# First batch of x in two halves, low weight parts of two more heads on VectorE, other banks for two chunks, later norms of x

## What is computed

```python
def ln(x): return (x - mean(x)) / sqrt(var(x) + 1e-5)          # over the 256 columns

n = ln(x)                                                       # x: (4, 256, 256)
q, k, v = (einsum('bim,mhd->bhid', n, w) for w in (wq, wk, wv)) # 16 heads of 128
q, k = rope(q), rope(k)
p = softmax(q @ k.T / 128 - 1e30 * (i < j))
x = x + ln(einsum('bhid,hdm->bim', p @ v, wo))
h = ln(x)                                                       # 1024 rows
r, chosen = top_k(h @ router.T + router_bias, 4); w = softmax(r)
gate, up = (h @ gate_up[e] + b)[0::2], [1::2]                   # for each chosen expert e
gate, up = min(gate, 7), clip(up, -7, 7)
y = sum over e of w[e] * ((up + 1) * gate * sigmoid(1.702 * gate) @ down[e] + down_bias[e])
x = x + ln(y)
```

## Time and profile before

| | us |
|---|---|
| median of 3 runs | 497.1 |
| lowest and highest | 496.76, 497.86 |
| the profiled execution | 498.67 |
| its span (first to last instruction) | 496.7 |
| PE busy in it | 470.8 |
| DVE, ACT, POOL busy | 359.4, 326.9, 240.9 |

### The profile page before, as it was taken

One profiled execution on the slowest core, in us unless ns is written; L12 is line 12 of the kernel. 1 busy time (PEld: TensorE's weight loads), 2 busy tenths in 40 slices (PEclk: granted clock), 3 DMA queues, 4 the chain that ended last, 5 costly groups with the idle time before them and its releaser, 6 DMA issues. The chain is left out here.

```text
span 496.7 us, 11704 instructions
## 1 busy us (share of the span) xinstructions
PE 470.8 (95%) x3482; PEld 439.7 (89%) x3482; DVE 359.4 (72%) x1263; ACT 326.9 (66%) x815; POOL 240.9 (49%) x228
## 2 busy tenths in 40 slices
PE   7799999999999999999999999998699999999993
PEld 4698899999999999999999998887589999999983
DVE  3798799687876677787678698577367778866735
ACT  4878986767676777667678566675256765665612
POOL 2888785435323256344453236115435565665612
PEclk9999999999999999999999999999799999999998
DMA  8367751999300000001365346631275665776462
GB/s 255 105 197 231 227 175 49 373 368 370 108 1 1 23 14 37 36 14 38 131 221 197 128 145 215 204 88 71 46 160 93 103 97 98 116 123 79 46 188 86
DMA packets 61661, 65.26 MB, mean 131 GB/s; under 512 B 4960, under 2 KB 56480, under 8 KB 61600
## 3 DMA queue, kind: packets, MB, share of 16 engines
q1 hardware_dynamic: 53008, 53.44, 33.6%
q0 software_dynamic: 7872, 10.49, 12.7%
q10 hardware_dynamic: 720, 0.59, 0.4%
HBM read 31.58 MB, written 32.92 MB: 130 GB/s over the span
## 5 line engine op out<-in xcount | busy, mean ns | idle before, releaser
L527 POOL TENSOR_TENSOR by_sin<-by_sin,rope_sin 128x512 f32<-128x512 f32 x64 | 82.8, 1294 | 139.9 <-ACT by_sin L649 139.9
L1343 PE MATMUL bank<-xT_parts,qk_h 128*128 128x256 f32 x512 | 99.6, 293 | 3.8 <-POOL qk_l L512 1.6
L1544 PE MATMUL bank<-xgT,gu_now 128*128 128x128 f32 x752 | 94.1, 279 | 7.2 <-DVE gu_now L1146 6.3
L1544 PEld LDWEIGHTS bank<-xgT,gu_now 128*128 128x128 f32 x752 | 89.4, 195 | 8.9 <-DVE gu_now L1146 7.0
L649 ACT ACTIVATE by_sin<-bank 64x512 f32<-64x512 f32 x128 | 75.9, 593 | 31.8 <-PE bank L1343 29.0
L625 POOL DMA_INDIRECT sum_d<-y,xg x44 | 69.9, 1589 | 55.0 <-ACT y L777 35.8
L1343 PEld LDWEIGHTS bank<-xT_parts,qk_h 128*128 128x128 f32 x512 | 79.1, 191 | 5.0 <-POOL qk_l L512 2.4
L671 ACT ACTIVATE prob<-score,row_bias 128x128 f32<-128x128 f32 (+1 forms) x128 | 57.0, 447 | 26.7 <-DVE row_bias L974 26.4
L1343 PE MATMUL bank<-xT_parts,qk_l 128*128 128x256 f32 x256 | 72.4, 283 | 0.0
L1343 PE MATMUL bank<-wv_h,xT_parts 128*128 128x256 f32 x256 | 66.6, 324 | 1.5 <-ACT V L649 1.4
L964 DVE TENSOR_TENSOR qkT<-bank,by_sin 128x512 f32<-128x512 f32 x64 | 44.3, 692 | 18.0 <-POOL by_sin L527 15.3
(11 more groups left out here) (183 smaller groups left out, 1061.2 us busy)
## 6 DMA issues: line engine op xcount, KB each, us to landing
rows_d<-blank SPq DMA_DIRECT2D x32, 576.0 KB, 7.2
gu_w<-_L_ffn_gate_up_proj_dram SPq DMA_DIRECT2D x16, 512.0 KB
xg<-rows_d SPq DMA_DIRECT2D x47, 144.0 KB, 2.5
dn_w<-in_L_ffn_down_proj_dram SPq DMA_DIRECT2D x16, 256.0 KB
raw_qk<-in_L_attn_wq_dram SPq DMA_DIRECT2D x16, 128.0 KB, 3.6
raw_qk<-in_L_attn_wk_dram SPq DMA_DIRECT2D x16, 128.0 KB, 3.7
raw_v<-in_L_attn_wv_dram SPq DMA_DIRECT2D x8, 256.0 KB, 2.9
raw_o<-in_L_attn_wo_dram SPq DMA_DIRECT2D x16, 128.0 KB, 2.7
```

The lines of the kernel that those rows point to most:

```text
L527: pool.tensor_tensor(v, v, rope_sin[:, :].unsqueeze(1).broadcast_to([P, 2, T]), ALU.mult).then_inc(pool_sin, 1)
L1343: m = pe.matmul(out, lhs, rhs, start=first and i == 0, stop=last and i == len(terms) - 1, skip_group_check=not (first and last))
L1544: m = pe.matmul(ps_gu[i][:, (2 * s + r) * P:(2 * s + r + 1) * P], gu_now[:, i % 2, k, s, r * P:(r + 1) * P], xgT[:, i % XT, k, :], start=( ...
```

## The change

1. Batch 0 of x is loaded by two DMAs, one for each tile. Statistics, power, norm, transpose, high part and low part are done for each tile by itself, with two banks (`ps_first`). On ACT, `high_qk(0)` stands between the two norms. PE's fillers at the start are two products of 512 columns and one of 256, and two and three products of 128 columns behind the transposes of the halves.
2. `DVE_HEADS` is 4: DVE makes the low parts of wq and wk for heads 2 and 3 too.
3. Chunks 2 and 3 go to banks 7 and 6, and chunks 4 and 5 wait for `rotate(0)` and `rotate(1)`, where chunks 2 to 5 waited for `rotate(0)` to `rotate(3)`.
4. ACT's, POOL's and DVE's orders in the start are other ones. In the slots, POOL does `low_v` ahead of `low_o`.
5. The statistics of batches 1 to 3 of x are taken in slots 5, 10 and 12 (`X_SLOTS`), and ACT normalises them in slots 6, 11 and 13.

```diff
-        ps_qk = bank[0:2]
+        ps_qk = [bank[0], bank[1], bank[7], bank[6]] + [bank[n % 2] for n in range(4, SLOTS)]
...
+        ps_first = [ps_s, ps_pT]
...
-        DVE_HEADS, DVE_PAIRS = 2, 1
+        DVE_HEADS, DVE_PAIRS = 4, 1
+
+        X_SLOTS = (5, 10, 12)
...
-            load_x(0)
+            for s in range(2):
+                sp.dma_start(x[:, s, :], x_rows[:, s, :]).then_inc(dma_first_x[s], 16)
...
             pool.wait_ge(dma_rope, 32)
             times_sine(0)
             times_sine(1)
-            low_qk(3)
+            low_qk(4)
+            times_sine(2)
             low_v(1)
-            times_sine(2)
-            low_qk(4)
+            times_sine(3)
             low_qk(5)
-            times_sine(3)
             low_o(0)
...
                 if b == 0:
+                    if h % 2 == 1 and h // 2 + 2 < H // 2:
+                        low_v(h // 2 + 2)
                     if h + 1 < H:
                         low_o(h + 1)
-                    if h % 2 == 1 and h // 2 + 2 < H // 2:
-                        low_v(h // 2 + 2)
-                    if h in (1, 2, 3):
-                        power("x", h)
+                    if h in X_SLOTS:
+                        power("x", X_SLOTS.index(h) + 1)
...
-            normalise("x", 0, xn, x)
+            first_norm(0)
             high_qk(0)
-            sc.wait_ge(pe_xT, 1)
-            copy(xT_h[:, 0, :, :], ps_s[:, :].rearrange("p (k t) -> p k t", k=KM)).then_inc(act_xT, 1)
+            first_norm(1)
+            first_xT_high(0)
+            first_xT_high(1)
             high_qk(1)
             high_v(0)
             high_qk(2)
             swap(0)
             high_qk(3)
             swap(1)
+            high_qk(4)
             values(0)
+            swap(2)
             high_v(1)
-            swap(2)
-            high_qk(4)
+            softmax_exp(0)
             swap(3)
+            softmax_exp(1)
             high_qk(5)
-            softmax_exp(0)
-            softmax_exp(1)
...
-                    if h in (4, 5, 6):
-                        normalise("x", h - 3, xn, x)
+                    if h - 1 in X_SLOTS:
+                        normalise("x", X_SLOTS.index(h - 1) + 1, xn, x)
...
-                if n >= 2:
-                    pe.wait_ge(dve_rope, n - 1)
+                if n >= 4:
+                    pe.wait_ge(dve_rope, n - 3 if n < 6 else n - 1)
...
-            keep_busy(qkT[:, 0, 0, 0:P], qkT[:, 0, :, :].rearrange("p w t -> p (w t)"), 4)
+            keep_busy(qkT[:, 0, 0, 0:P], qkT[:, 0, :, :].rearrange("p w t -> p (w t)"), 2)
+            keep_busy(qkT[:, 0, 0, 0:P], qkT[:, 0, 0, :], 1)
             pe.wait_ge(dma_ident, 16)
-            pe.wait_ge(act_norm, 1)
-            turn_rows(0, ps_s).then_inc(pe_xT, 1)
+            for s in range(2):
+                pe.wait_ge(act_first_norm[s], 1)
+                for k in range(KM):
+                    m = pe.transpose(ps_first[s][:, k * P:(k + 1) * P], xn[:, s, k * P:(k + 1) * P], ident[:, :])
+                m.then_inc(pe_first_xT[s], 1)
+                keep_busy(qkT[:, 0, 0, 0:P], qkT[:, 0, 0, 0:P], 2 + s)
```

More of the change, by code:

```diff
@@ L209, in block_kernel @@
         ps_sum = bank[6:8] + bank[0:2]
-        dma_x = [sem(f"dma_x{u}") for u in range(4)]
+        ps_first = [ps_s, ps_pT]
+        dma_x = [None] + [sem(f"dma_x{u}") for u in range(1, 4)]
+        dma_first_x = [sem(f"dma_first_x{s}") for s in range(2)]
         dma_ident = sem("dma_ident")
+        dve_first_var = [sem(f"dve_first_var{s}") for s in range(2)]
+        dve_first_mean = [sem(f"dve_first_mean{s}") for s in range(2)]
+        pool_first_rstd = [sem(f"pool_first_rstd{s}") for s in range(2)]
+        pool_first_shift = [sem(f"pool_first_shift{s}") for s in range(2)]
+        act_first_norm = [sem(f"act_first_norm{s}") for s in range(2)]
+        pe_first_xT = [sem(f"pe_first_xT{s}") for s in range(2)]
+        act_first_xT = [sem(f"act_first_xT{s}") for s in range(2)]
         dma_rope = sem("dma_rope")
@@ L268, in block_kernel @@
         dve_var = sem("dve_var")
+        dve_mean = sem("dve_mean")
         dve_xT = sem("dve_xT")
@@ L317, in block_kernel @@
         pe_y = sem("pe_y")
-        NORMS = ([("x", u) for u in range(B)] + [n for u in range(B) for n in (("a", u), ("b", u))]
+        NORMS = ([("x", u) for u in range(1, B)] + [n for u in range(B) for n in (("a", u), ("b", u))]
                  + [("moe", u) for u in range(B)])
@@ L561, in tables @@
                     pool.memset(tile_edge[:, 0:1], -1.0).then_inc(pool_table, 1)
-            power("x", 0)
-            low_qk(2)
+            for s in range(2):
+                pool.wait_ge(dve_first_var[s], 1)
+                pool.tensor_tensor(first_rstd[:, s:s + 1], first_eps[:, s:s + 1], minus_half[:, 0:1], ALU.pow).then_inc(pool_first_rstd[s], 1)
+                pool.wait_ge(pool_first_rstd[s], 1)
+                pool.wait_ge(dve_first_mean[s], 1)
+                pool.tensor_tensor(first_shift[:, s:s + 1], first_mean[:, s:s + 1], first_rstd[:, s:s + 1], ALU.mult).then_inc(pool_first_shift[s], 1)
             pool.wait_ge(dma_rope, 32)
@@ L1175, in _, with first_stats, first_xT_low @@
             dve.memset(qkT[:, 0, :, :], 0.0).then_inc(dve_idle, 1)
-            dve.wait_ge(dma_x[0], 16)
-            row_stats(x, "x", 0)
+            def first_stats(s):
+                dve.wait_ge(dma_first_x[s], 16)
+                chain(dve.bn_stats(stats[:, s, :], x[:, s, :]))
+                chain(dve.bn_aggr(mean_var[:, s, :], stats[:, s, :]))
+                dve.tensor_scalar(first_eps[:, s:s + 1], mean_var[:, s, 1:2], EPS, None, ALU.add).then_inc(dve_first_var[s], 1)
+                dve.tensor_scalar(first_mean[:, s:s + 1], mean_var[:, s, 0:1], -1.0, None, ALU.mult).then_inc(dve_first_mean[s], 1)
+            def first_xT_low(s):
+                dve.wait_ge(act_first_xT[s], 1)
+                cols = slice(s * P, (s + 1) * P)
+                m = dve.tensor_tensor(xT_l[:, 0, :, cols], ps_first[s][:, 0:KM * P].rearrange("p (k t) -> p k t", k=KM),
+                                      xT_h[:, 0, :, cols].bitcast(F32), ALU.subtract)
+                if s == 1:
+                    m.then_inc(dve_xT, 1)
+            first_stats(0)
+            first_stats(1)
             low_qk(0)
-            xT_low(0, ps_s)
+            first_xT_low(0)
+            first_xT_low(1)
             low_qk(1)
             low_v(0)
+            low_qk(2)
             dve.wait_ge(dma_rope, 32)
             cosine(0)
+            low_qk(3)
             rotate(0)
@@ L1190, in _ @@
             cosine(2)
+            row_max(1)
+            normalise_prob(0)
             rotate(2)
             cosine(3)
-            row_max(1)
-            normalise_prob(0)
             rotate(3)
```

39 lines of the change are left out of this document (27 added, 12 removed).

## The result

The changed kernel takes 495.42 us, median of 8 runs (494.51 to 496.18); the kernel before took 497.25 beside it, median of 8 (496.14 to 499.24). The ratio is 0.9959, with a 95% interval of 0.9945 to 0.9974: 1.3 to 2.7 us less. The forecast was 493.0, a gain of 4.1 us; the measured gain is 1.8. The sign was right, and 495.42 lies within the stated range, near its upper end. The profiled execution of the changed kernel took 495.41, with a span of 493.4.

The account below looks back on a forecast made before the run. TensorE was taken as the bound, busy 95% of the span, so only its waits could be won. 1.95 us from the start plus 2.1 from the ten slots gave 4.05 off the 497.1 median: 493.0 us, range 491.4 to 495.9.

Parts of the forecast that it names:

- What bounds the kernel: Whole kernel: TensorE is busy 95% of the span, so only time in which it waits can be won.
- First product, 0.15 earlier: Start of attention: PE's first product at 9.75 instead of 9.91 us, between 0.35 later and 0.9 earlier.
- weigh_values(0) at 23.7: End of the start: first weigh_values 2.15 us before 25.85, with ACT as bound; bounds 1.3 and 2.8.
- Slots 1 and 2, 1.95 left: Slots 1 and 2: weigh_values(2) ends at 34.3 instead of 36.2, keeping 1.95 of the start's 2.15 us.
- Order on POOL and later norms, 2.1 us: Ten slots from 38.00 to 87.01: low_v first and later norms win 2.1 of 3.1 us of waits; bounds 0 and 3.1.
- The ring: Two-slot wait cycle through single buffer raw_v over ACT and POOL: 10.2 us against PE's 9.0, falling to 8.5.
- The range: Whole kernel's time: 491.4 to 495.9 us.
- the start's lower bound: Least gain at the first weigh_values, 1.3 us, from more ACT waits for weights; total given as 495.9.
- Rival B, the clock: Start: thinner warm-up leaves PE at the lower clock, losing 1.25 to 2.1 us; 494.7 us, chance 0.20.
- Rival C: Slots: waits for raw_v stay, as ACT or its load is late; only 1.95 us won, 495.1, chance 0.13.
- Rival D: Expert stage: one more PE hold of 4.3 us with its cold stretch; slower, 500.4 us, chance 0.08.
- Rival E: No change: worst cold start (2.1) together with raw_v waits that stay; 0.15 earlier, 497.0 us, chance 0.09.

Follow-up runs that it names:

- halves_alone: Kernel before with only the first batch of x normalised and turned as two halves, and the shorter fillers; ratio 1.0009 to the kernel before.
- start_alone: Kernel before with four heads on DVE, chunks 2 and 3 in banks 7 and 6, and the new orders ahead of the slots; ratio 1.0053.
- ring_undone: Changed kernel with POOL's low_o put back ahead of low_v in the slots; ratio 0.9960 to the kernel before.
- norms_early: Changed kernel with the norms of x back at statistics in slots 1, 2, 3 and ACT's part in 4, 5, 6; ratio 0.9966 to before.
- start_and_ring: Kernel before with four heads on DVE, banks 7 and 6, the new start orders, and low_v ahead of low_o in POOL's slots; ratio 0.9959.
- norms_in_batch_1: Changed kernel with the second and third norms of x later: statistics in slots 14 and 20, ACT's part in 15 and 24; ratio 0.9918 to before.
- change_again: The changed kernel run once more, with no edit; ratio 0.9965 to the kernel before.
- later_and_no_double: Changed kernel with second and third norms at slots 14/15 and 20/24, and slot 10's qk_l of head 15 behind the sine product; ratio 0.9933.

## Why the prediction was right or wrong

**What bounds the kernel: right.** What the edits moved, they moved before 90 us, and the distance from slot 13 to the last scores was the same in each of fourteen traces: a lead at slot 13 was kept whole.

**First product, 0.15 earlier: mis-sized, without effect.** It came 1.00 us earlier (9.71 to 8.88 in the traces of the change's start at the full clock with halves, against 9.91). The forecast took wk's landing at its slowest, 5.4 us after an issue at 1.75, thus 7.15. Behind the additional load of x it was issued at 2.17, and high_qk(0) could start at 6.27; in the second trace it waited until 7.07. The first norm was forecast at 5.45, from an arrival at 3.5 that mixes a time with durations counted from the issue at 0.73; the half was there by 3.32 and the norm started at 5.17. The bound of 0.9 was given. But the term was not in the sum, as ACT was the bound, and halves_alone confirms that.

**weigh_values(0) at 23.7: right.** 23.67 in the profile. One trace of before overstates the gain a little: four traces with the old order of the start have 25.39 to 25.85, mean 25.55, nine with the new one at the full clock 23.31 to 23.98, mean 23.74. That is 1.8 us rather than 2.15. GPSIMD Engine Reference in the Trainium skill, section 8, speaks of contention between the two engines without a price; the 0.2 us for each subtraction on POOL that the prediction took for it from the earlier trace rows did not appear: qk_l took 1.29 and 1.28 us. Where the two did meet, in start_alone, it was DVE's subtraction that was held: 1.27 us at 13.48 instead of 0.69, beside POOL's sine product.

**Slots 1 and 2, 1.95 left: right.** 1.86. That this works only with the rest of the change is what start_alone shows: with the old places and the old ring the lead is gone by slot 3. The part that counts here is the norms' place: from w0 to slot 3 the change takes 12.47 us and ring_undone 12.48, but norms_early and start_and_ring, with the new ring and the norms in their old slots, 13.70 and 13.72. The prediction does not say that this term, 1.2 us of its 1.95, depends on the norms having left slots 1 to 3.

**Order on POOL and later norms, 2.1 us: wrong, and the cause of the miss.** It was 0.4 us (49.01 to 48.61). The ring did what was said. The view of wv_h on ACT in the kernel before:

```profile
L649 ACT ACTIVATE wv_h<-raw_v x8: 620/632/632, 9.5 to 75.8; 128x512 fp32r<-128x512 f32 x8
...
  DMA raw_v<-in_L_attn_wv_dram: 3.0, 4
```

and in the changed one:

```profile
L670 ACT ACTIVATE wv_h<-raw_v x7: 619/629/633, 17.2 to 71.6; 128x512 fp32r<-128x512 f32 x7
...
  DMA raw_v<-in_L_attn_wv_dram: 0.8, 2
```

3.0 us of waiting fell to 0.8, and slots 3 to 10 won 1.50. The size of this term is what failed, and the step is the sentence "From slot 10 on no head's weights are prepared, so ACT and DVE have room of over 0.5 us in each slot". In slot 10 DVE has none: POOL still makes the low part of head 15's weights there (slot h prepares head h + 5), next to the sine product; the parts of wv for the last pair and of wo are made in slots 10 and 11 too. The multiply beside POOL's two operations takes 2.7 us, in the trace of before as well. With the statistics put behind it (1.13 us) and the norm into slot 11 (1.08 us), the two slots lost 1.10 us; how much of that is each one's is open. Without the second and third norm there the ten slots take 47.16 and 47.22 us, 1.8 won, which is near the 2.1 forecast, and the ratio is 0.992 to 0.993, where the forecast's 493.0 was 0.992 of 497.1.

**The range: it held, but not by the sum.** The sum's own bounds, 2.4 to 5.7 us won, end at 494.7, and 495.42 lies outside. The lower one does not follow from its terms either: 1.3 less the 0.2 of slots 1 and 2, and 0 for the ten slots, give 1.1 us. It is the rivals and the start's lower bound that carried the range to 495.9.

**Rival B, the clock: not in the profiled execution, but real.** In the change's trace the transposes take 0.66 us at 5.91, still at the lower level, and 0.44 at 7.45, and from there to the last scores the granted clock is 1.00. In norms_in_batch_1's trace, whose start is the change's, it was 1.00 up to 8.2 us, where PE had just stood still for 1.49 us for the second norm, and 0.50 from 8.3 to 11.6, so that the first products ran at half speed. PE's timeline from 8 to 11 us:

```profile
8.14 0.64 PE L1631 MATMUL bank<-ident,xrow 128*128 128x128 f32 x2 [1.49 <-ACT xrow L809]
8.58 1.48 PE L1570 MATMUL bank<-qkT 128*128 128x128 f32 x6
9.81 0.77 PE L1399 MATMUL bank<-xT_parts,qk_h 128*128 128x256 f32 x2
```

and the same kernel's table of stretches (length, busy us and instructions of PE, PEld, DVE, ACT and POOL, granted clock, DMA share, GB/s):

```profile
7.00:8.20 1.20, 0.06 (x1) 0.06 (x1) 0.57 (x1) 1.20 (x3) 0.00 (x0) 1.00 1.05 318
8.30:11.60 3.30, 3.30 (x16) 3.29 (x16) 2.71 (x6) 2.00 (x5) 0.00 (x0) 0.50 1.05 331
11.70:15.00 3.30, 3.30 (x29) 3.30 (x29) 1.36 (x2) 2.60 (x5) 1.30 (x1) 1.00 0.72 191
```

The mechanism was right and its price too high. Here wk landed late as well (high_qk(0) at 6.97), so the like cases are change_again and later_and_no_double, with the first product at 9.71 and 9.62 at the full clock and w0 at 23.97 and 23.98: against them w0 came at 24.31, so 0.3 us was lost and not 1.25 to 2.1. In change_again PE stood still for 1.03 us in the same place, and the clock stayed at 1.00. The late wk is what opens the gap; of nine traces with the halves and the shorter fillers this is the only one in which the clock fell. Here 2.4 GHz is the 1.00 and 1.2 GHz the 0.50.

**Rival C: its number, not its cause.** It gave 495.1, and 495.4 was measured, but the ring did go. **Rival D** did not come: the holds are 1.09 and 4.89 us now, 5.98 in sum against 6.27, one cold stretch as before. But such holds come and go between executions without any edit, as said below. **Rival E** did not come.

The time after the last scores, 172 to 182 us, varies by more than all that was sought here, and the traces show where. In six of them (before, the change, and the four of the third group) PE stands still for 1.1 to 2.0 us near 341 to 345 and for 4.3 to 4.9 us near 349 to 352, with a cold stretch behind: 180.3 to 181.8 us. Seven (three of the first group, four of the second) have neither hold and take 172.4 to 174.8; change_again's, with 180.2 us, has neither hold, but a mean granted clock of 0.97 from 370 to 484 us, where the other traces of its group and the second have 0.99 or 1.00. The kernel before belongs to the long ones in its trace, but its medians of 490.35 and 490.36 beside those groups fit the 490 that the prediction named for the case that the fall of the clock vanishes. What stays open is what brings the two holds: DVE and ACT, for which PE waits in the second, wait for something that the profile does not name. Open is also how often the clock falls at the start, since only profiled executions show it.

## What to carry to other kernels

Before work is moved into a slot "with room", read that slot's own row on the engine that will carry it, and look who is queued behind it: average load says little where two engines slow each other down, and a short job on the critical path (here the row maximum) is as late as everything that stands ahead of it on its engine. Changes to one pipeline share their costs: the start by itself made the kernel slower, with either of two remedies it was 0.4% faster than before, and the remedies together were hardly better than each; a part tested alone tells its price only beside the others. And a step that is won ahead of the bound, as the first product was here, is worth nothing until the bound itself moves.
